# A 16-item early-fusion network on one core: where the first mixture's expert weights are split in two halves of precision

## The reference

```python
patches = _patchify(x, P)                                   # 16 x 36 x 768
h = silu(patches @ W1 + b1) @ W2 + b2                       # tokens of the pictures
h = concatenate([h, txt], axis=1)                           # 16 x 113 x 256
h = h + _L0_attn_ref(_layernorm(h, axis=-1), ...)           # a selective scan: h_t = exp(dt A) h + dt B x, y = C h
h = h + _L0_ffn_ref(_layernorm(h, axis=-1), ...)            # 15 experts, 3 picked per token, and a shared one
```

## Time and profile before

| | us |
|---|---|
| median of three runs | 1495.68 |
| lowest, highest | 1491.24, 1498.45 |
| the profiled execution | 1503.98 |
| its span | 1502.2 |

### The profile page before, as it was taken

How to read it: one execution, slowest core, us unless ns; L and a number is a source line. 1 busy time by engine, 2 the same in 40 slices (tenths; PEclk the granted TensorE clock), 3 DMA queues, 4 the chain that set the end, 5 groups by cost and what they waited for, 6 DMA issues and landing times. The chain is left out here.

```text
span 1502.2 us, 31497 instructions
## 1 busy us (share of the span) xinstructions
PE 1071.6 (71%) x9872; PEld 748.8 (50%) x9872; DVE 1050.2 (70%) x2316; ACT 723.5 (48%) x1444; POOL 503.5 (34%) x644
## 2 busy tenths in 40 slices
PE   4637788774299998577666977266579996379991
PEld 2222233224288875354444764144456664378881
DVE  3968999987555554565986764778758886745553
ACT  4666555553265543224445742144358886234440
POOL 0063777762254553731001100000026665232204
PEclk9558999995599999887888979689769997589996
DMA  6600000001344544312000000000023331112214
GB/s 196 231 12 1 0 1 1 0 1 50 99 122 138 157 131 154 95 43 85 0 1 0 1 1 1 0 1 0 0 72 113 111 112 52 50 55 64 64 50 122
DMA packets 47766, 89.68 MB, mean 60 GB/s; under 512 B 8352, under 2 KB 34629, under 8 KB 46789
## 3 DMA queue, kind: packets, MB, share of 16 engines
q1 hardware_dynamic: 40578, 67.98, 14.7%
q0 software_dynamic: 6912, 18.88, 4.5%
q10 hardware_dynamic: 144, 1.05, 0.2%
HBM read 71.84 MB, written 16.04 MB: 59 GB/s over the span
## 5 line engine op out<-in xcount | busy, mean ns | idle before, releaser
L1190 POOL TENSOR_TENSOR scan_ch<-scan_hs,scan_ct 128x452 f32<-128x452 f32 x128 | 143.4, 1141 | 75.1 <-DVE scan_hs L1300 51.3
L1213 PE MATMUL scan_py<-scan_ch,ident 128*128 128x452 f32 x256 | 131.7, 605 | 40.8 <-POOL scan_ch L1190 31.3
L1300 DVE TENSOR_TENSOR_SCAN scan_hs<-scan_abar,scan_bx 128x452 f32<-128x452 f32 x128 | 133.2, 1084 | 0.5 <-ACT scan_abar L1262 0.3
L458 PE MATMUL m0x_ph<-m0x_xb,m_w_hi 128*128 128x128 f16 x456 | 99.9, 221 | 1.2 <-ACT m0x_xb L1962 1.0
L459 PE MATMUL m0x_ph<-m0x_xb,m_w_hi 128*128 128x128 f16 x456 | 99.9, 221 | 0.0
L460 PE MATMUL m0x_ph<-m0x_xb,m_w_lo 128*128 128x128 f16 x456 | 99.6, 220 | 0.0
L2027 DVE TENSOR_SCALAR m3x_a<-m3x_ph,m3x_b 128x128 f32<-128x128 f32 x184 | 49.6, 342 | 70.0 <-ACT m3x_ah L1988 70.0
L1213 PEld LDWEIGHTS scan_py<-scan_ch,ident 128*128 128x128 f32 x256 | 41.1, 194 | 111.3 <-POOL scan_ch L1190 100.7
L1262 ACT ACTIVATE scan_abar<-ssm_dt,ssm_a 128x448 f32<-128x448 f32 x128 | 80.9, 640 | 22.9 <-DVE scan_hs L1300 21.6
L2024 DVE SCALAR_TENSOR_TENSOR m0x_a<-m0x_ph,m0x_b,m0x_gate 128x128 f32<-128x128 f32 x114 | 34.7, 346 | 72.4 <-issue 36.7
L1988 ACT ACTIVATE m3x_ah<-m3x_ph,m3x_b 128x128 f16<-128x128 f32 x184 | 50.3, 386 | 65.7 <-PE m3x_ph L460 61.7
(11 more groups left out here) (691 smaller groups left out, 3822.9 us busy)
## 6 DMA issues: line engine op xcount, KB each, us to landing
mha_wbuf<-m3w SPq DMA_DIRECT2D x32, 512.0 KB, 3.7
tok_wbuf<-m0w SPq DMA_DIRECT2D x15, 768.0 KB, 5.4
m0x_b<-m0b SPq DMA_DIRECT2D x57, 128.0 KB
m_out<-m0x_yo SPq DMA_DIRECT2D x57, 128.0 KB
m3x_b<-m3b SPq DMA_DIRECT2D x23, 128.0 KB, 3.0
m_out<-m3x_yo SPq DMA_DIRECT2D x23, 128.0 KB
m_rows<-m0r_parts SPq DMA_DIRECT2D x4, 448.0 KB
m_rows<-m3r_parts SPq DMA_DIRECT2D x4, 448.0 KB
```

The lines of the kernel that those rows point to most:

```text
L458: pe.matmul(out, w_hi, x_hi, start=start, stop=False)
L1190: pool.tensor_tensor(ch[r][:], hs[r][:], ct[n % 2][:], ALU.mult).then_inc(weighed, 1)
L1213: pe.matmul(py[c][:, 0:GT], core.ident[:], ch[u % R][:], start=n == 0, stop=n == NS - 1).then_inc(summed, 1)
L1300: dve.tensor_tensor_scan(hs[u % R][:], abar[c][:, 0:GT], bx[u % R][:], 0.0, ALU.mult, ALU.add).then_inc(scanned, 1)
```

## The change

- In the token stage `b2` is no longer split: it is loaded once per row (36 rows) and added by VectorE in the copy of each token group, and the two one-row matmuls go. TensorE waits for three split weights.
- The text is loaded after the experts.
- Only 11 of the 15 experts are loaded and split in this stage. `scale_small` goes to the head of VectorE's stream, behind the weights' split. Experts 0 and 1 are split before unit 0, and one more before each of the units 1 to 3 (on ScalarE before the unit's Silu, on VectorE before its `g_lo`). The other six follow the units; VectorE does one after each of the first six copies, and then makes the last ten copies. The loops are written out.
- Experts 11 to 14 are split in the scan stage by the new `LatePieces`, in 12 pieces of 128x512 (two of the first matrix and one of the second for each expert), with three buffers. SyncE loads them (256 KB each). ScalarE, behind state 2, 6, 10 and 14 of a group, makes the high half and then scales the piece in place; GpSimd, behind state 3, 7, 11 and 15, subtracts. The twelve pieces take the first three groups.
- `gain` moves from the stage's tiles to those of the mixture.

```diff
--- before.py
+++ after.py
@@ -489,7 +489,7 @@
         pt_hi, pt_lo = st.sb("pt_hi", [128, PC, NP], F16), st.sb("pt_lo", [128, PC, NP], F16)
         w1_hi, w1_lo = st.sb("w1_hi", [128, PC, D], F16), st.sb("w1_lo", [128, PC, D], F16)
         w2_hi, w2_lo = st.sb("w2_hi", [128, KC, D], F16), st.sb("w2_lo", [128, KC, D], F16)
-        b2_hi, b2_lo = st.sb("b2_hi", [1, D], F16), st.sb("b2_lo", [1, D], F16)
+        b2 = st.sb("b2", [LP, 1, D])
         b1 = st.sb("b1", [128, KC])
         g = st.sb("g", [128, KC, NP])
         g_hi, g_lo = st.sb("g_hi", [128, KC, NP], F16), st.sb("g_lo", [128, KC, NP], F16)
@@ -507,24 +507,33 @@
             ("w1", d["w1"], w1_hi[:].rearrange("p c n -> p (c n)"), w1_lo[:].rearrange("p c n -> p (c n)")),
             ("pt", d["patches"], pt_hi[:].rearrange("p c n -> p (c n)"), pt_lo[:].rearrange("p c n -> p (c n)")),
             ("w2", d["w2"], w2_hi[:].rearrange("p c n -> p (c n)"), w2_lo[:].rearrange("p c n -> p (c n)")),
-            ("b2", d["b2"], b2_hi[:], b2_lo[:]),
         ])
         units = [(c, s) for c in range(KC) for s in range(2)]
+        BEFORE = (2, 3, 4, 5)
+        step_at = lambda n: At(n // 4, n % 4)
         with nc.Block() as block:
             @block.sync
             def _(sp):
                 w_sync(sp)
                 sp.dma_start(b1[:], d["b1"]).then_inc(consts, 16)
+                sp.dma_start(b2[:].rearrange("p a n -> p (a n)"), d["b2"].to_broadcast([LP, D])).then_inc(consts, 16)
+                mw.load_small(sp)
+                for n in range(m.steps - m.late):
+                    mw.load(sp, step_at(n))
                 sp.dma_start(core.h[LP:L, :, :], d["txt"]).then_inc(text, 16)
-                mw.load_small(sp)
-                steps(sp, m.steps, lambda at: mw.load(sp, at))
                 sp.wait_ge(text, 16)
             @block.scalar
             def _(act):
                 w_act(act)
-                act.wait_ge(consts, 16)
+                act.wait_ge(consts, 32)
+                act.wait_ge(mw.ready, 2)
+                made = 0
                 for n, (c, s) in enumerate(units):
+                    for made in range(made, BEFORE[n]):
+                        mw.high(act, step_at(made))
+                    made = BEFORE[n]
                     act.wait_ge(hid_ready, n + 1)
                     act.activation(g[:, c, s * HP:(s + 1) * HP], hid[n % 2][:, 0:HP], ACT.Silu, bias=b1[:, c:c + 1],
                                    scale=1.0 / (WS * WS)).then_inc(hid_free, 1)
@@ -532,31 +541,31 @@
                     act.wait_ge(hid_free, n + 1)
                     act.activation(g_hi[:, c, s * HP:(s + 1) * HP], g[:, c, s * HP:(s + 1) * HP],
                                    ACT.Copy).then_inc(g_high, 1)
-                act.wait_ge(mw.ready, 2)
-                steps(act, m.steps, lambda at: mw.high(act, at))
+                for n in range(made, m.steps - m.late):
+                    mw.high(act, step_at(n))
             @block.vector
             def _(dve):
                 w_dve(dve)
+                mw.scale_small(dve)
+                made = 0
                 for n, (c, s) in enumerate(units):
+                    for made in range(made, BEFORE[n]):
+                        mw.low(dve, step_at(made))
+                    made = BEFORE[n]
                     dve.wait_ge(g_high, n + 1)
                     dve.tensor_tensor(g_lo[:, c, s * HP:(s + 1) * HP], g[:, c, s * HP:(s + 1) * HP],
                                       g_hi[:, c, s * HP:(s + 1) * HP], ALU.subtract).then_inc(g_split, 1)
-                mw.scale_small(dve)
-                def copy_tokens(at):
-                    p, before = at.of(2)
-                    dve.wait_ge(emb_ready[p], before + 1)
-                    dve.tensor_scalar(core.h[0:LP, bass.ds(at.j, 1), :], emb[p][0:LP, :].unsqueeze(1),
-                                      1.0 / WS, None, ALU.mult).then_inc(emb_free[p], 1)
-                def step(at):
-                    copy_tokens(at)
-                    mw.low(dve, at)
-                steps(dve, m.steps, step)
-                for j in range(m.steps, NB):
-                    copy_tokens(At(0, j))
+                dve.wait_ge(consts, 32)
+                for j in range(NB):
+                    p = j % 2
+                    dve.wait_ge(emb_ready[p], j // 2 + 1)
+                    dve.scalar_tensor_tensor(core.h[0:LP, j:j + 1, :], emb[p][0:LP, :].unsqueeze(1), 1.0 / WS, b2[:],
+                                             ALU.mult, ALU.add).then_inc(emb_free[p], 1)
+                    if made + j < m.steps - m.late:
+                        mw.low(dve, step_at(made + j))
             @block.tensor
             def _(pe):
@@ -576,11 +585,9 @@
                         pe.wait_ge(emb_free[j], i)
                         tok = bass.ds(i * (2 * LP) + j * LP, LP)
                         for k in range(KC):
-                            mm3(pe, emb[j][0:LP, :], g_hi[:, k, tok], g_lo[:, k, tok],
-                                w2_hi[:, k, :], w2_lo[:, k, :], k == 0, False)
-                        pe.matmul(emb[j][0:LP, :], core.ones16[0:1, 0:LP], b2_hi[:], start=False, stop=False)
-                        pe.matmul(emb[j][0:LP, :], core.ones16[0:1, 0:LP], b2_lo[:], start=False,
-                                  stop=True).then_inc(emb_ready[j], 1)
+                            last = mm3(pe, emb[j][0:LP, :], g_hi[:, k, tok], g_lo[:, k, tok],
+                                       w2_hi[:, k, :], w2_lo[:, k, :], k == 0, k == KC - 1)
+                        last.then_inc(emb_ready[j], 1)
 def stage_norm_stats(nc, core, name, src):
@@ -1151,7 +1158,7 @@
                                           ALU.mult).then_inc(dx_done, 1)
-def stage_ssm_scan(nc, core, ssm):
+def stage_ssm_scan(nc, core, ssm, m, d):
@@ -1168,6 +1175,8 @@
          added) = (st.sem(n) for n in ("zeroed", "b_ready", "c_ready", "c_copied", "decay", "drive",
                                        "scanned", "weighed", "summed", "y_out", "turned", "added"))
+        late = LatePieces(st, m, d)
         def groups(eng, body):
@@ -1175,6 +1184,11 @@
                 body(q, q > 0)
         with nc.Block() as block:
+            @block.sync
+            def _(sp):
+                for t in range(late.pieces):
+                    late.load(sp, t)
             @block.gpsimd
             def _(pool):
                 def body(q, behind):
@@ -1188,6 +1202,8 @@
                             need(pool, summed, m - (R - 1))
                             pool.wait_ge(scanned, m + 1)
                             pool.tensor_tensor(ch[r][:], hs[r][:], ct[n % 2][:], ALU.mult).then_inc(weighed, 1)
+                        if n % 4 == 3 and (q * NS + n) // 4 < late.pieces:
+                            late.low(pool, (q * NS + n) // 4)
                 groups(pool, body)
@@ -1264,6 +1280,8 @@
                                            ACT.Exp, scale=ssm.a[:, c * NS + n:c * NS + n + 1]).then_inc(decay, 1)
                         if n == 1 and behind:
                             copy_out(q - 1)
+                        if n % 4 == 2 and (q * NS + n) // 4 < late.pieces:
+                            late.split(act, (q * NS + n) // 4)
                 groups(act, body)
                 copy_out(NG - 1)
@@ -1347,6 +1365,7 @@
         self.halves = 2 if KC * in_chunks * 128 > 1024 else 1
         self.steps = experts * self.halves
+        self.late = 4 if gelu else 0
     def buffers(self, nc, ctx, weights):
@@ -1354,6 +1373,7 @@
             return ctx.enter_context(nc.sbuf_tensor(f"{self.name}_{name}", shape, dt))
         self.b1 = sb("b1", [128, self.E, self.NF], F32)
+        self.gain = sb("gain", [128, self.E, self.FH], F32) if self.mult else None
         self.router_hi, self.router_lo = (sb(n, [128, KC * self.E], F16) for n in ("router_hi", "router_lo"))
         self.weight, self.slot = sb("weight", [L, NB, self.K], F32), sb("slot", [128, NB, self.K], U32)
         self.ids, self.expert = sb("ids", [128, self.blocks], U32), sb("expert", [1, self.blocks], I32)
@@ -1394,7 +1414,7 @@
     def small_tiles(self, st):
         m = self.m
         if m.mult:
-            self.gain = st.sb("gain", [128, m.E, m.FH])
+            self.gain = m.gain
         self.router = st.sb("router", [128, KC * m.E])
     def parts(self, at, w1, w2):
@@ -1455,6 +1475,54 @@
             ins = dve.scalar_tensor_tensor(dst, src.rearrange("p (a n) -> p a n", a=1),
                                            WS if g is None else g, hi, ALU.mult, ALU.subtract)
         ins.then_inc(self.lo_done[b], 1)
+class LatePieces:
+    COLS, DEPTH = 512, 3
+    def __init__(self, st, m, d):
+        self.m, self.d = m, d
+        self.pieces = m.late * 3
+        self.buf = [st.sb(f"piece{p}", [128, self.COLS]) for p in range(self.DEPTH)]
+        self.landed = [st.sem(f"piece_landed{p}") for p in range(self.DEPTH)]
+        self.hi_done, self.scaled, self.lo_done = st.sem("piece_hi"), st.sem("piece_scaled"), st.sem("piece_lo")
```

(34 more changed lines are left out.)

## The result

The changed kernel takes 1485.07 us in the median of six runs (1480.35 to 1486.91), the kernel before 1496.27 in six (1491.24 to 1498.45): a ratio of 0.9925, with a 95% interval from 0.9905 to 0.9945. That is 11.2 us less, 0.75%.

What follows compares the result with a forecast made beforehand. VectorE was taken to set the pace in the token stage and the scan. -10.5 us (token stage) + 0 (scan) took the profiled 1503.98 to 1493.5; the runs' median, 8.3 lower, gave 1485.2 us, range 1479 to 1496.

Steps and rivals of the forecast that it cites:

- (1): Token stage, TensorE's gate: without b2's split the last weight piece is ready at 18.28, patch layer starts 0.35 us earlier.
- (2): Token stage, text behind the experts: small loads land six microseconds earlier, ScalarE can start an expert at 18.5.
- (3): Token stage, five experts before and between the units: last g_lo ends at 34.9, embeddings start 3.05 us later.
- (4): Token loop: first token near 36.4, six experts at 2.26 us to 50.0; loads of experts 9 and 10 just in time.
- (5): Token tail, ten copies without experts: TensorE bounds, four tokens slow and four fast, stage ends at 59.7, 10.5 us earlier.
- rival (a): Token tail stays at half clock or loads of experts 9 and 10 come late: saving 7 to 8.5 us; chance 0.25.
- cost 0: Scan: the twelve late pieces cost VectorE 0 us, bound above by 30 with bursts fully exposed.
- the 2.1 read off the timeline: Scan, ScalarE: 0.83 us idle and 1.28 ahead leave 2.1 us for a burst, once in four steps.
- the argument for GpSimd: Scan: a 1.1 us subtraction after every fourth step fits in GpSimd's idle time and makes one product 0.3 late.
- 3.2 in four: Scan, GpSimd: 0.81 us idle a step, taken as 3.2 us over four steps for one subtraction.
- The other half: Scan, GpSimd: the C copy two steps on and VectorE's four-deep buffers leave time for a product 0.3 late.
- Rival (b): Scan: ScalarE's bursts reach VectorE, all 17 us (chance 0.05) or a part, 3 to 10 us (chance 0.12).
- rival (c): Token loop paced by loads, 3.3 us an expert instead of 2.26: stage ends at 65.9, saving 4.3 us; chance 0.1.

Runs made afterwards that it cites:

- act_burst: Changed kernel with ScalarE's high half of each late piece made three times; scan 212.68 us against 205.72 in the changed kernel.
- pool_burst: Changed kernel with GpSimd's subtraction of each late piece made three times; scan 220.04 us against 205.72 in the changed kernel.
- text_first: Changed kernel with the text loaded ahead of the small tensors and experts; next stage starts at 61.52 us against 59.31.
- spread_low: Changed kernel with an expert's low part behind every second copy instead of every copy; 1479.21 us, ratio 0.9895 to the kernel before.
- no_late: Changed kernel with all 15 experts in the token stage and the scan untouched; 1491.58 us, ratio 0.9962 to the kernel before.
- units_first: Changed kernel with two experts ahead of the first unit and none between units; next stage starts at 60.48 us against 59.31.
- before_again: The kernel before, unchanged, profiled a second time; next stage starts at 68.48 us against 70.56 in its first profile.
- b2_matmuls: Changed kernel with b2 added by the two one-row matmuls again and a plain copy; next stage starts at 64.46 us against 59.31.
- late_only: Kernel before with only the late pieces added: 11 experts in the token stage, four split in the scan; 1498.97 us, ratio 1.0002 to before.

## Why the prediction was right, and where its terms were off

The median moved by 11.2 us where 10.5 were forecast (1485.07 against 1485.2, since the later runs of before had a median 0.6 higher), and by the mechanism named. The closeness is in part luck. The 11.25 us are taken from one profile of each kernel. act_burst and pool_burst have the changed kernel's token stage too, and the next stage starts at 58.91 and 59.09 in them, 59.1 in the mean of three; before's two are 70.56 and 68.48. By these means the stage is 10.4 us shorter. By the prediction's steps:

(1) and (2) hold. TensorE's patch layer started at 18.51, not 18.3, and ScalarE's first expert at 18.71, not 18.5. Why the text mattered was partly wrong: expert 0's load would have been even later than the small tensors (text_first). Its worth there was 2.2 us. The small tensors' b1 took 6.6 us to land instead of 14.7, eight sooner, not the six of the estimate.

(3) was 0.9 too long: the last `g_lo` ended at 33.97, not 34.9. ScalarE's table load ran right behind expert 1, at 22.33, and not behind the wait for the first unit, forecast for 22.9, which makes 0.6; each further unit with its expert took 2.60 us instead of 2.74, which makes 0.4. TensorE's earlier full clock was not the cause: in spread_low it came 5.7 us after the first matmul instead of 2.85, and the table load was still at 22.48, ahead of the first unit's last matmul at 22.71, and the last `g_lo` ended at 34.13. The two experts ahead of the unit were free, as said.

(4) is right in length: 35.89 to 49.67 is 13.78 against 13.6. The margin of the loads of experts 9 and 10 was as thin as stated: ScalarE idled 2.95 and 1.47 us for them, VectorE 0.2 for the later one. The last copy of the phase stands 0.3 earlier than forecast.

(5) is the step that carried the forecast and it held. TensorE restarted at 50.22 and ran at half clock for four tokens (50.22 to 55.3), then full; the stage's last copy ended at 59.00 against 59.7. A token at half clock took 1.28 us where 1.35 was priced. The choice of the unbroken patch layer as the nearest row, rather than of the loop's own half clock, was the right one: rival (a) would have had 61.9. That the clock took 5.3 us to come back, so near to the 5.5 of that row, was luck: in the other tails of six matmuls a token it took 2.9 (text_first), 3.4 (no_late), 3.8 (units_first), 4.7 (act_burst) and 5.7 us (pool_burst), and text_first's tail was 1.1 us shorter for it.

In the loop, with one token's matmuls in each 2.26 us, the clock went both ways: full at 38.70, half at 45.47. The Trainium skill ("TensorE: Matmul & The Clock Gate", part 1, What's actually happening), cited in the prediction, says that activity releases the clock; the tail agrees, the loop does not bear it out as it stands.

The scan: cost 0 was right (0.1 in the mean of the profiles, 0.3 in the first pair). ScalarE's room was 2.35 us against the 2.1 read off the timeline. Half of the argument for GpSimd fails: "3.2 in four" steps is not room, as pool_burst shows, where subtractions of 3.6 us, only just over it, cost 1.2 a piece. The other half holds: the 1.16 us make one product 0.3 late, and the C copy and the 1.3 us that the next decay is ahead leave time for that.

Rival (b) would have needed bursts over 2.35 us; act_burst put them there and they cost 7 us. Of rival (c), two loads came late and cost 0.2 us.

The profiled executions differ by 23.6 us, twice the change of the median. 11.25 are the token stage, 2.1 us more than against before_again. 1.8 are the scan's inputs (62.61 and 60.77 us), a stage that takes 60.1 to 61.0 or 62.1 to 62.8 us in the thirteen profiles, and 10.8 lie behind the scan, where nothing was edited. There, from the route stage to the end, the thirteen profiles run from 1152.8 to 1163.6, both kernels among them, and the unchanged kernel itself gave 1163.6 and 1156.8. One part is seen: 102.8 us for the first profile's shared expert stage, 93.9 to 96.2 in all others. What makes these stages vary wasn't isolated.

## What to carry to other kernels

When work is taken out of a loop in which two engines overlap, the other engine is bare for as many turns as were removed: price those turns from its own rows (here 1.28 us at half clock, about 0.75 at full), and then spread what is left so that neither stands alone, which here was worth another 4.2 to 5.3 us of the stage. Work slipped behind the pace-setting engine of a pipeline fits if one burst is shorter than the idle time at that place plus the lead of its next product; the idle time summed over several steps is not room. And a difference of single profiles should be split by stage, and the kernel before profiled twice, before it is believed: of 23.6 us at most 11.3 were the change.

## What the runs showed of the hardware that was not expected

TensorE's clock depended on how it was fed in the token loop. In the changed kernel's loop, with one token's six matmuls in each 2.26 us and pauses of 1.43, it was full at 38.70 and half again at 45.47; in spread_low, with two tokens in each 2.6 us and pauses of 1.11, it stayed full from 38.10 to the end of the stage. Whether the shorter pauses or the greater amount of work made the difference is not shown, since both changed.

The first rise came 2.85 us after the first matmul in the changed kernel (18.51 to 21.36), 5.5 us after it in the first profile of the kernel before and 4.3 in the second, for the same matmuls; the thirteen profiles run from 2.85 to 5.7. In the tails it ran from 2.9 to 5.7 us with six matmuls a token; with eight, two of them of one row, it was 9.3 us in b2_matmuls, and in the two profiles of late_only's kernel the clock did not come back before the end, 5.5 us on. A forecast that leans on the moment of the rise is uncertain by that much.
